# A one-core transformer block on Trainium2: bias wait, result adds, routing steps and extra products placed anew

## The reference, cut to what matters

```python
x = x + _L0_attn_a_ref(_layernorm(x), ...)   # x: (16, 256, 128), 16 heads of 8, latent 32, rotary, causal
x = x + _L0_ffn_ref(_layernorm(x), ...)      # experts, see below
x = x + _L0_attn_b_ref(_layernorm(x), ...)   # plain causal attention, 16 heads of 8
x = x + _L0_ffn_ref(_layernorm(x), ...)      # the same experts again

# _L0_ffn_ref: 8 experts, 4096 tokens, the best two of each token
logits = flat @ gate_w + gate_b
topv, topi = lax.top_k(logits, 2)
topw = softmax(topv)
for e in range(8):                           # F = 512
    h = gelu(flat @ W1[e] + b1[e], approximate=False)
    acc += (h @ W2[e] + b2[e]) * routing[:, e][:, None]
```

## Time and profile before

| | us |
|---|---|
| timed runs | 1198.99, 1195.26, 1197.36 (median 1197.36) |
| profiled execution | 1191.1 |
| its span, first to last instruction | 1189.4 |
| PE busy in the span | 1024.3 (86%) |
| POOL / DVE / ACT busy | 758.7 / 747.3 / 648.2 |
| mean granted TensorE clock | 0.908 of full |

### The profile page before, as it was taken

One profiled execution on the slowest core, in us unless ns is written; L12 is line 12 of the kernel. 1 busy time (PEld: TensorE's weight loads), 2 busy tenths in 40 slices (PEclk: granted clock), 3 DMA queues, 4 the chain that ended last, 5 costly groups with the idle time before them and its releaser, 6 DMA issues. The chain is left out here.

```text
span 1189.4 us, 29763 instructions
## 1 busy us (share of the span) xinstructions
PE 1024.3 (86%) x11227; PEld 793.5 (67%) x11227; DVE 747.3 (63%) x1845; ACT 648.2 (55%) x1193; POOL 758.7 (64%) x824
## 2 busy tenths in 40 slices
PE   4799999999988987999877899999988878999820
PEld 3566776676765666999874556666655557999820
DVE  5878888888889954622345677777777626322332
ACT  1476777776755543455445667767755424455410
POOL 2788988888876746277663477667534233577765
PEclk9799999999998897999997999999988658999975
DMA  9100011010000023578940000000000024688732
GB/s 263 4 2 20 19 38 37 20 37 16 6 11 2 11 72 93 162 232 251 217 121 1 1 15 24 25 16 23 13 8 4 10 98 133 182 239 222 241 104 68
DMA packets 69805, 91.10 MB, mean 77 GB/s; under 512 B 15074, under 2 KB 49762, under 8 KB 69666
## 3 DMA queue, kind: packets, MB, share of 16 engines
q1 hardware_dynamic: 58226, 68.98, 18.4%
q0 software_dynamic: 9088, 18.63, 7.3%
q10 hardware_dynamic: 2352, 1.58, 0.5%
HBM read 68.45 MB, written 20.71 MB: 75 GB/s over the span
## 5 line engine op out<-in xcount | busy, mean ns | idle before, releaser
L1417 ACT ACTIVATE PT<-PS 128x768 f32<-128x768 f32 x256 | 207.1, 809 | 133.0 <-PE PS L1925 79.2
L608 POOL TENSOR_SCALAR_AFFINE_SELECT PT<-PT 128x512 f32<-128x512 f32 x256 | 179.4, 701 | 144.1 <-ACT PT L1417 143.5
L621 POOL DMA_INDIRECT xg<-normed,source x156 | 148.0, 949 | 94.8 <-DVE source L1101 48.1
L1448 ACT ACTIVATE hid<-PS,b_cols 128x256 f32<-128x256 f32 x312 | 122.5, 475 | 113.3 <-PE PS L1664 110.5
L1983 PE MATMUL PS<-W,hid 128*128 x1248 | 158.9, 283 | 0.1
L1983 PEld LDWEIGHTS PS<-W,hid 128*128 128x128 f32 x1248 | 152.6, 199 | 0.6 <-issue 0.5
L730 POOL DMA_INDIRECT got<-expert_rows,slot_of x128 | 122.7, 959 | 40.2 <-issue 34.4
L1311 DVE TENSOR_TENSOR y_rows<-PS,b_rows 128x256 f32<-128x256 f32 x78 | 33.1, 425 | 149.0 <-PE PS L1983 144.1
L1755 PE MATMUL PS<-PT,v_aug 128*32 128x256 f32 (+1 forms) x2048 | 117.9, 352 | 2.2 <-POOL PT L608 2.1
L1737 PE MATMUL PS<-causal_b,ident_b 128*128 128x256 bf16 x512 | 104.1, 287 | 13.5 <-DVE q_aug L1260 12.9
L1662 PE MATMUL PS<-xg_hi,w_ring 128*128 128x256 f32 x312 | 96.9, 311 | 16.7 <-DVE xg_lo L1167 13.0
(11 more groups left out here) (301 smaller groups left out, 2993.2 us busy)
## 6 DMA issues: line engine op xcount, KB each, us to landing
w_ring<-halves_w SPq DMA_DIRECT2D x78, 512.0 KB
expert_rows<-y_rows SPq DMA_DIRECT2D x78, 128.0 KB, 3.1
normed<-xn SPq DMA_DIRECT2D x16, 256.0 KB, 2.3
xg<-normed,source POOLq DMA_INDIRECT x156
W<-in_L_ffn_w_dram SPq DMA_DIRECT2D x1, 2048.0 KB, 13.8
halves_w<-w_hi SPq DMA_DIRECT2D x8, 256.0 KB, 2.3
halves_w<-W SPq DMA_DIRECT2D x8, 256.0 KB, 2.0
got<-expert_rows,slot_of POOLq DMA_INDIRECT x128, 2.7
```

The costliest lines, as they stand in the source:

```text
L608: nc.gpsimd.affine_select(out=diagonals, in_=diagonals, pattern=[[0, 4], [1, P]], compare_op=ALU.is_ge, fill=0.0, base=0, channel_multipli ...
L621: nc.gpsimd.indirect_dma_start(out=xg[:, i % AHEAD, b_, :], out_offset=None, in_=normed if i >= EARLY else normed[0:NH * P, :], in_offset= ...
L1417: s.activation(PT[:, unit % 2, pair, :, :, :], PS[:, 4:6, 0:3 * P].rearrange("p h (a q) -> p a h q", q=P), ACT.Exp).then_inc(m["exp_done"], 1)
L1448: ins = s.activation(hid[:, r % 2, k, :], h_bank[r % 2][k // 2][:, k % 2 * ROWS:(k % 2 + 1) * ROWS], ACT.Gelu, bias=b1_cols[:, bass.ds(e * ...
```

## The change

The wait for b2 moves from in front of the tile loop to just before the first `finish`. ADDED_AT becomes FIRST_DONE + 7 = 30, so tiles 30 to 38 add 27 results; the last five, and the weights of the second half, go into `last_results`, which in stage "1" is called in attention b's prologue behind its first step, and in stage "2" right behind the loop. The statistics move with ADDED_AT, and ACT's first layer norm of attention b stands one tile earlier. From unit 47 of attention b on DVE takes its routing piece ahead of the `late` closing. And PE gets a new piece in units 56 to 63, `unread`: three matmuls of 512 columns into bank 7, whose result nobody reads, in the place of the missing `early` step, once the bank's last reader has freed it.

```diff
--- before.py
+++ after.py
@@ -38,7 +38,7 @@
 EARLY = -(-(2 * NH * P - E * (ROWS - 1)) // ROWS)
 FIRST_DONE = 2 * NH * P // ROWS + E - 1
 FIRST_BLOCKS = FIRST_DONE * RB
-ADDED_AT = FIRST_DONE + 5
+ADDED_AT = FIRST_DONE + 7
 ADDS = 3
 RESULTS = 8 * CT
 TABLE_AT = 5
@@ -295,8 +295,10 @@
 def adds_in(i):
 
     k = ADDS * (i - ADDED_AT)
-    end = RESULTS if i == TILES - 1 else min(k + ADDS, RESULTS)
-    return range(k, end) if i >= ADDED_AT else range(0)
+    return range(k, k + ADDS) if i >= ADDED_AT else range(0)
+
+
+ADDED = ADDS * (TILES - ADDED_AT)
 
 
 def split_at(unit):
@@ -1263,6 +1265,8 @@
                 own.then(v.memset(M[:, :, :], 0.0))
                 for s in plan.prologue:
                     closing(m, w, s, False)
+                    if s is plan.prologue[0]:
+                        last_results("1")
                     if (s.kind, s.g) == ("key", 0):
                         row_max(m, 0, 3 * HD)
                 for unit in range(NCH * UNITS):
@@ -1277,6 +1281,8 @@
                         closing(m, w, plan.early[unit], False)
                     if unit + 1 < NCH * UNITS:
                         row_max(m, unit + 1, 3 * HD)
+                    if unit > plan.ROUTE:
+                        route_first(m, w, moe_sems["2"], plan, unit)
                     if plan.late[unit]:
                         closing(m, w, plan.late[unit], False)
                     if c == 0:
@@ -1295,7 +1301,8 @@
                             tile_statistics(c - 1, range(CT), 1)
                         if u == 7:
                             end_statistics(m, 1)
-                    route_first(m, w, moe_sems["2"], plan, unit)
+                    if unit <= plan.ROUTE:
+                        route_first(m, w, moe_sems["2"], plan, unit)
                 close(m, w, plan, "b")
 
             def experts(n):
@@ -1339,12 +1346,13 @@
                         dve.wait_ge(m["table_ready"], 1)
                         sources(m, y_bank[(TABLE_AT + 1) % 2][:, 0:BLOCKS])
 
-                dve.wait_ge(m["bias_ready"], 16)
                 for i in range(TILES):
                     if i + 2 < TILES:
                         split_rows(m, i + 2)
                     if i <= TABLE_AT:
                         route_second(i)
+                    if i == 0:
+                        dve.wait_ge(m["bias_ready"], 16)
                     finish(i)
                     if i == TABLE_AT + 1:
                         weigh(0, m)
@@ -1355,8 +1363,12 @@
                     if n == "1" and i == ADDED_AT + 6:
                         dve.wait_ge(m["got_used"], 4 * CT)
                         statistics(att_sems["b"], 1, 1)
-                dve.wait_ge(m["got_used"], RESULTS)
-                weigh(1, m)
+
+            def last_results(n):
+
+                add_results(n, range(ADDED, RESULTS))
+                dve.wait_ge(moe_sems[n]["got_used"], RESULTS)
+                weigh(1, moe_sems[n])
 
             def add_results(n, rows):
 
@@ -1383,6 +1395,7 @@
             experts("1")
             attention_b()
             experts("2")
+            last_results("2")
             for c in range(RESULTS // (2 * CT), NCH):
                 add_expert_rows("2", c, range(2 * CT))
 
@@ -1596,7 +1609,7 @@
                         gelu(m, i + 1)
                     if i == TILES - 2:
                         gap_exponent(n, 1)
-                    if n == "1" and i == TILES - 2:
+                    if n == "1" and i == TILES - 3:
                         normal("b", 0, 1, 0)
 
 
@@ -1932,6 +1945,12 @@
                     b_, g = divmod(u, G)
                     weighted(m, unit, g, b_, g // 2 * S)
 
+                def unread(last):
+
+
+                    pe.wait_ge(m["freed_act" if last.by_act else "freed_dve"], last.freed)
+                    product(bank[7], w["hi"][0][:, 0:P], w["lo"][0][:, 0:P], x_hi[:, 1, :], x_lo[:, 1, :])
+
                 causal(range(4))
                 for s in plan.prologue:
                     step(s)
@@ -1946,6 +1965,8 @@
                         causal((2, 3))
                     if plan.early[unit]:
                         step(plan.early[unit])
+                    elif unit >= end - UNITS:
+                        unread(next(s for u in range(unit - 1, 0, -1) for s in (plan.extra[u], plan.late[u], plan.early[u]) if s))
                     if unit + 1 < end:
                         pe.wait_ge(m["aug_ready"], unit + 1)
                         causal((0, 1))
```

## The result

The changed kernel took 1180.97 us (median of 4 runs, 1178.17 to 1182.47) against 1198.17 for the kernel before: ratio 0.985, 95% interval 0.981 to 0.989. The same kernel timed again later gave 0.984 (0.980 to 0.988). The forecast was 1175.5. The profiled execution of after took 1180.08 us with a span of 1178.3, that is 11.1 us less than the span before.

A forecast was written before the change was run, and what follows sets the result against it. PE bounds the expert stages apart from waits; POOL's gathers and DVE's adds fill the last 49.4 us. 6.5 + 1.0 + 4.1 + 5.1 + 2.0 + 3.0 = 21.7 us off 1191.1, plus 6.3 to the median: 1175.5, range 1164 to 1189.

The forecast's parts named there:

- Part 1: Start of both expert stages: moving the b2 wait removes PE's stalls, gain 6.5 us, plus 1 for the clock.
- Part 2: Tile 28, both stages: adds from tile 30 remove PE's stalls of 4.85 and 5.06 us; stage "1" counted in Part 3.
- Rival D: Tile 30: gather landing moves with the tile, DVE waits as at 28, Parts 2 and 3 give 0; 1184.9 us, chance 0.09.
- Part 3: Border to attention b: first scores come earlier, gain 4.1 us, containing stage "1"'s 4.85 less 0.75 given back.
- Part 4: Attention b's end: routing before the closing lets weight loads start some 4.5 us earlier, gain 2 us.
- Part 5: Units 56 to 63: unread products fill PE's gaps and the clock rises after a few units, gain 3 us.
- B: Units 56 to 63: the products don't raise the clock and cost 6.7 us; 1185.4 us, chance 0.20.
- C: Clock up from unit 56 or 57 to the units' end: 8.3 us instead of 3; 1168.9 us, chance 0.15.

The follow-up runs named there:

- e1: The kernel before with only the wait for b2 moved to the first finished tile: ratio 0.992 against before.
- e3: The changed kernel with empty row-list slots pointing to rows of their own instead of all to row 0: ratio 0.976 against before.
- e4: The changed kernel without the unread products: ratio 0.989 against before.
- e7: The kernel before with only the empty row-list slots pointing to rows of their own: ratio 0.991 against before.
- e2: The kernel before with only the later adds, last results behind attention b's first tile and ACT's norm one tile earlier: ratio 1.000 against before.
- e6: The kernel before with only the unread products: ratio 0.993 against before.
- e5: The kernel before with only the routing ahead of the closing in the units after 46: ratio 0.992 against before.
- e11: e3 with tiles 22 to 24 reading only row 0 in stage "1" and rows 0 to 7 in stage "2": timed once, 1176.36 us.

## Why the prediction came out near

The time lay in the forecast's range, 5.5 us above its value, but of five steps two failed, two were too small, and one gave back part of what it won. That the sum came near is in part luck: the clock gain that was missing from parts 4 and 5 stood in for some of what parts 2 and 3 never gave.

- **Part 1, right about the wait, too large in the gain.** Forecast 6.5 and 1 for the clock; turns 0 to 8 give 6.4 in e1, 2.5 + 1.6 and 2.5 + 2.6 in the two profiles of after. The step that failed is "so I let nothing come late": PE now waits for the split behind the first `finish`, 1.45 and 2.13 us. In e3 and e4 PE then meets the next limit, the gathers that need the second row list (3.1 us of waiting in e3): counted to turn 10, their stage "2" takes 54.9 and 54.7 us against 55.4 before and 51.8 in e1.
- **Part 2, wrong at its first sentence.** "DVE reaches the first add after tile 28 and stands 5.46 us ... Its next split comes late, and PE stalls." For stage "1" that is not what PE's own row says. Before, PE stood first and longer for the weights:

```profile
580.79 0.35 PE L1662 MATMUL PS<-xg_hi,w_ring 128*128 128x256 f32 x1 [3.51 <-issue]
...
585.29 0.36 PE L1662 MATMUL PS<-xg_hi,w_ring 128*128 128x256 f32 x1 [0.85 <-DVE xg_lo L1167]
```

  The split held it for 0.85 us. In stage "2" PE did wait for the split, 3.24 us, of which the split alone was worth half at most, since the last completion of the weights came only at 1106.35, 1.66 us into that wait:

```profile
1107.93 0.55 PE L1662 MATMUL PS<-xg_hi,w_ring 128*128 128x256 f32 x1 [3.24 <-DVE xg_lo L1167]
```

  but with that wait away the weight loads are late next (20.2 - 17.1 = 3.1 us lost in after, 1.8 in e1, which left the adds). Both waits were symptoms of one slow stretch of the DMA engines, which I had as a given latency of 11.5 us. I treated the other landing of 2.54 us at the border as the exception, when it was the rule (3.6 in e3).
- **The Trainium skill on DMA.** The fit of the Trainium skill, "DMA: Bandwidth & Descriptors", anatomy of a GpSimd DMA, gives an estimate of 2.15 us for a 64 KB gather. I set it aside for the rows of 11.5 us. With the slots mended they land after 3.6 us: nearer to the fit, and by it tile 28 doesn't wait, as in e7.
- **Rival D** names the right result for parts 2 and 3, zero, and the wrong mechanism: by its own proof, a wait before the first add of tile 30, it is refuted in stage "1" (590.51) and in stage "2", where that add stands behind no wait either (1101.83).
- **Part 3, wrong.** Forecast 4.1, measured 0.2 (30.0 and 29.8) in the first profile of after and -1.3 in the second, and nothing in e2's time. It drew 4.85 us from the stall, which stayed. And qs starts after the last add, at 629.83, where the keys were ready at 629.05 (POOL's last: 627.80 + 1.25).
- **Part 4, too small.** Forecast 2. The distance to turn 0 of "2" fell by 1.9, and units 47 to 55 by 1.4 (the q_aug of unit 47 lies 46.9 and 45.5 us ahead of that of 55). What I missed is the clock: this order alone shortens units 55 to 63 by 4 to 7.5 us (43.7 against 47.5, 51.1 and 51.2).
- **Part 5, right in kind and too small.** Forecast 3, alone 9 (by the profile 5 to 9). B, that the clock wouldn't rise, is refuted by e6. C, the fast clock throughout, is nearer in its mechanism than I had it, 0.88 over units 56 to 63, though its time, 1168.9, is not. What I missed in the sum is that parts 4 and 5 lift the clock of the same units: I had them as two gains, and the main part of it can be won once only. The Trainium skill, "TensorE: Matmul & The Clock Gate", What's actually happening, says that activity releases the throttle; by itself that doesn't tell e1 from e5, which issue the same 328 matmul records there at 0.54 and 0.72.
- **The sum.** 9.2 us of parts 2 and 3 were not there; attention b and the way to turn 0 of "2" gave 8.4 (2.2 + 4.3 + 1.9) instead of 5, and part 1 some 4 to 6.4. That makes 12 to 15 of the 17.2 us timed, whose interval is 13.4 to 22.6. The profiled pair shows only 11.1: its stage "1" lost 3.1 us more at turns 29 to 34 than the one of before, which had the smallest such stall of all the profiles here without the mend.

## What to carry to other kernels

When an engine stands still, read its own row and ask what it waited for before blaming the longest wait beside it; two waits at one time often have one cause, and moving one of them only shows the other. When a transfer is slow at one place only, look at what shares the DMA engines there, and at what the indices of unused slots point to: give them different rows. Pieces that each lift the clock of the same stretch need not add up, so time them alone and together. And when a wait is moved, look at what now stands behind it: here two new waits of PE took back part of the gain.

## What the runs showed of the hardware

- Gathers that read one 512 byte row in all 128 lanes are slow and slow SP's stores and weight loads beside them: 0.84 us per packet against 0.11 (e11), 87 to 127 GB/s at a busy share of 0.9 to 1.09 (before, after, e11) against 225 to 255 at 0.77 to 0.85 (e11's stage "2", e3), stores landing after 11.6 us instead of 3.2, and SP's issue of a weight load taking up to 3.32 us instead of 0.34 (after against e3). Eight rows in the place of one show nothing of it (e11).
- Units that keep PE busy for 38 of 42 us ran at a granted clock of 0.62 (before), and others that keep it busy for 32 of 36 at 0.78 (e4): the share of busy time doesn't tell which clock a stretch gets.
